# Block numbers earlier and in small portions, result stores from ScalarE's queue

## The reference

```python
shared = gelu(x2 @ Ws1 + bs1) @ Ws2 + bs2
y = shared
y = y + _bank_residual(x2, Wr_sp, br_sp, W1_sp, b1_sp, W2_sp, b2_sp)
y = y + _bank_residual(x2, Wr_fq, br_fq, W1_fq, b1_fq, W2_fq, b2_fq)
# _bank_residual, 8 experts, each 512 -> 128 -> 512, no row is over capacity here:
expert = argmax(softmax(x2 @ Wr + br)); gate = its probability
h = gelu(buf[expert] @ W1[expert] + b1[expert])
y = (h @ W2[expert] + b2[expert]) * gate
```

## Time and profile before

| | |
|---|---|
| median of 3 runs | 516.19 us |
| profiled execution | 513.78 us, span 512.0 us |
| TensorE busy | 458.2 us (89%), 2602 matmuls |
| VectorE, ScalarE, GpSimd busy | 212.8, 167.4, 176.0 us |
| DMA | 121.37 MB, mean 237 GB/s |
| y_dram<-ybuf | 18 stores of 256 KB, median 7.9 us to landing |
| x_raw<-x_dram | 12 loads of 256 KB |
| got<-y_dram | 10 gathers, GpSimd idle 43.0 us before them, 40.3 of it for a store of ybuf |

### The profile page before, as it was taken

One profiled execution on the slowest core, in us unless ns is written; L12 is line 12 of the kernel. 1 busy time (PEld: TensorE's weight loads), 2 busy tenths in 40 slices (PEclk: granted clock), 3 DMA queues, 4 the chain that ended last, 5 costly groups with the idle time before them and its releaser, 6 DMA issues.

```text
span 512.0 us, 7417 instructions
## 1 busy us (share of the span) xinstructions
PE 458.2 (89%) x2602; PEld 321.3 (63%) x2602; DVE 212.8 (42%) x518; ACT 167.4 (33%) x365; POOL 176.0 (34%) x198
## 2 busy tenths in 40 slices
PE   2799799989999998889999999999999996998980
PEld 2354447767665654666577877777777784864660
DVE  4779971212451728452221012420025595422226
ACT  2699673313210112720231032340064502243300
POOL 3102000083500802495325825206036339500081
PEclk9999999999999999999999999999999999999986
DMA  5999999969999879777504460210011016999965
GB/s 122 397 424 419 426 424 357 324 236 321 408 396 426 303 239 424 298 260 244 196 1 123 164 246 1 38 69 5 1 58 45 0 31 200 321 390 405 402 172 162
DMA packets 40164, 121.37 MB, mean 237 GB/s; under 512 B 7402, under 2 KB 7463, under 8 KB 31678
## 3 DMA queue, kind: packets, MB, share of 16 engines
q1 hardware_dynamic: 36766, 117.01, 61.0%
q0 software_dynamic: 3360, 3.86, 2.9%
HBM read 106.02 MB, written 14.82 MB: 236 GB/s over the span
## 4 chain that ended last, share of the span: by engine, by line
PE 70%; issue 9%; DVE 5%; POOL 5%; DMA 4%; ACT 3%; DVEq 1%; SPq 1%; POOLq 0%
PE ps L1601 13%; PE ps L1603 11%; PE ps L1602 11%; PE ps L1625 10%; PE ps L1960 9%; PE ps L1686 5%; PE ps L1805 2%; DMA y_dram<-ybuf 2%; ACT h_tmp L1347 1%; POOL sort L817 1%; DMA x_raw<-x_dram 1%; PE ps L2075 1%; POOL x_dram L846 1%; PE ps L1609 1%; DMA got<-y_dram,slot_u 1%
## 5 line engine op out<-in xcount | busy, mean ns | idle before, releaser
L1625 PE MATMUL ps<-ring,sel_att 128*32 128x512 f32 x512 | 66.0, 602 | 6.0 <-DMA ring<-in_L_gnn_basis_dram 2.4
L1601 PE MATMUL ps<-piece_hi,ht_hi 128*125 128x512 f32 x140 | 56.1, 401 | 0.8 <-PE ps L1603 0.6
L1602 PE MATMUL ps<-piece_lo,ht_hi 128*125 128x512 f32 x140 | 55.1, 394 | 0.0
L1603 PE MATMUL ps<-piece_hi,ht_lo 128*125 128x512 f32 x140 | 55.1, 394 | 0.0
L1084 DVE SCALAR_TENSOR_TENSOR u_lo<-ps,gates,u_hi 125x512 fp32r<-125x512 f32 x20 | 15.0, 751 | 94.1 <-ACT u_hi L1493 94.1
L751 POOL CAST piece_hi<-piece_raw 128x512 fp32r<-128x512 f32 x28 | 19.8, 707 | 92.3 <-issue 53.7
L752 POOL TENSOR_TENSOR piece_lo<-piece_raw,piece_hi 128x512 fp32r<-128x512 f32 x28 | 37.8, 1349 | 13.3 <-issue 11.1
L934 DVE TENSOR_SCALAR oh_n<-iota_n,keys 125x626 f16<-125x626 f16 x100 | 38.7, 387 | 7.9 <-PE ps L1686 5.7
L1960 PE MATMUL ps<-u_hi,cf 125*125 125x512 f32 x100 | 39.9, 399 | 1.3 <-PE ps L1603 1.3
L1960 PE MATMUL ps<-u_lo,cf 125*125 125x512 f32 x100 | 39.4, 394 | 0.0
L1686 PE MATMUL ps<-oh_n,oh_m 125*128 125x313 f16 x200 | 31.3, 314 | 4.3 <-DVE oh_m L935 4.3
(11 more groups left out here) (332 smaller groups left out, 934.9 us busy)
## 6 DMA issues: line engine op xcount, KB each, us to landing
ring<-in_L_gnn_basis_dram SPq DMA_DIRECT2D x64, 1024.0 KB, 9.4
w_home<-in_L_ffn_W_sp_dram SPq DMA_DIRECT2D x27, 256.0 KB, 5.6
y_dram<-ybuf SPq DMA_DIRECT2D x18, 256.0 KB, 7.9
rel_dram<-stag SPq DMA_DIRECT2D x16, 256.0 KB, 8.3
w_raw<-rel_dram SPq DMA_DIRECT2D x8, 512.0 KB, 6.4
piece_raw<-in_L_mix_Wkqv_dram SPq DMA_DIRECT2D x3, 1024.0 KB, 10.6
x_dram<-stag SPq DMA_DIRECT2D x1, 3072.0 KB
w_home<-in_L_ffn_W_fq_dram SPq DMA_DIRECT2D x12, 256.0 KB, 5.9
```

Of the source, the lines that this page charges most:

```text
L1601: pe.matmul(target, a_hi, b_hi, start=first, stop=False, skip_group_check=skip)
L1602: pe.matmul(target, a_hi, b_lo, start=False, stop=False, skip_group_check=skip)
L1603: return pe.matmul(target, a_lo, b_hi, start=False, stop=last, skip_group_check=skip)
L1625: last = pe.matmul(ps[32 * c:32 * c + 32, rel_bank(ch), :], sel_att[:, ch // CHUNKS, g].rearrange("p r q -> p (r q)"), ring[slot][:, c * D ...
```

## The change

On VectorE the numbers of the blocks are made directly behind the slots; the three selections pick(0), pick(1) and pick(2), which stood between the steps of routing, come behind the transposed routes. ScalarE reads the first four numbers of bank 1 only after the Gelus of three tiles, and one number more in each loop turn. SyncE reads its numbers four at a time between weight loads, and three groups of weights come ahead of the row loads. The stores of bank 0's seven tiles and of bank 1's first seven blocks are issued by ScalarE in the loop; SyncE keeps the last five of bank 1. SyncE's `load_w2` comes one turn sooner.

```diff
--- before.py
+++ after.py
@@ -472,6 +472,11 @@
         def rel_bank(ch):
             return 3 + ch % 2 if ch < 2 * CHUNKS - 2 else 3
 
+        def store_block(queue, b, i):
+            queue.wait_ge(*y_done(b, i))
+            n = SB_FQ if b else y_rows(i)
+            queue.dma_start(y_dram[b][i * 128:i * 128 + n, :], ybuf[b][0:n, i, :]).then_inc(y_out[b], 16)
+
         block = ctx.enter_context(nc.Block())
 
 
@@ -585,10 +590,6 @@
             for n, a in enumerate((b2_sp, b2_fq)):
                 sp.dma_start(out_bias[n * E:(n + 1) * E, :], a).then_inc(smalls_in, 16)
             sp.dma_start(out_bias[2 * E:2 * E + 1, :], bs2.rearrange("(a n) -> a n", a=1)).then_inc(smalls_in, 16)
-            def store_block(b, i):
-                sp.wait_ge(*y_done(b, i))
-                n = SB_FQ if b else y_rows(i)
-                sp.dma_start(y_dram[b][i * 128:i * 128 + n, :], ybuf[b][0:n, i, :]).then_inc(y_out[b], 16)
             sp.wait_ge(zeroed, ZEROED)
             for n in range(RAWS, len(UNITS)):
                 load_unit(n)
@@ -638,37 +639,38 @@
                 sp.dma_start(x_raw[i % XRAWS][:], x_dram[i * SB_FQ:(i + 1) * SB_FQ, :]).then_inc(raw_in[i % XRAWS], 16)
             expert_of = {0: load_numbers(0, 4)}
             load_w2(0)
-            fq_of = load_numbers(NB, 4) + load_numbers(NB + 4, 4) + load_numbers(NB + 8, 4)
-            for i in range(3):
+            fq_of = load_numbers(NB, 4)
+            for i in range(4):
                 load_w1_fq(i)
+            expert_of[1] = load_numbers(4, 4)
+            load_w2(1)
             for i in range(XRAWS):
                 load_rows(i)
-            for i in range(3, W1S):
+            fq_of += load_numbers(NB + 4, 4)
+            for i in range(4, W1S):
                 load_w1_fq(i)
             for i in range(4, W2S):
                 load_w2_fq(i)
-            for j in range(1, NY):
-                expert_of[j] = load_numbers(4 * j, y_rows(j) // SB)
-            load_w2(1)
-            load_w2(2)
+            fq_of += load_numbers(NB + 8, 4)
+            for j in range(2, 4):
+                expert_of[j] = load_numbers(4 * j, 4)
+                load_w2(j)
             for i in range(4):
                 load_w2_fq(i)
+            for j in range(4, NY):
+                expert_of[j] = load_numbers(4 * j, y_rows(j) // SB)
             for i in range(XRAWS, NB_FQ):
                 load_rows(i)
                 if i - XRAWS + W1S < NB_FQ:
                     load_w1_fq(i - XRAWS + W1S)
-                if i - 2 < NY:
-                    load_w2(i - 2)
+                if i - 1 < NY:
+                    load_w2(i - 1)
                 if i >= XRAWS + 3:
                     load_w2_fq(i - XRAWS - 3 + W2S)
-                    store_block(0, i - XRAWS - 3)
-                    store_block(1, i - XRAWS - 3)
-            for i in range(NB_FQ - XRAWS - 3, NB_FQ):
-                if i + W2S < NB_FQ:
-                    load_w2_fq(i + W2S)
-                if i < NY:
-                    store_block(0, i)
-                store_block(1, i)
+            for i in range(NB_FQ - XRAWS - 3, NB_FQ - W2S):
+                load_w2_fq(i + W2S)
+            for i in range(NY, NB_FQ):
+                store_block(sp, 1, i)
             for t in range(NT):
                 sp.wait_ge(final_ready, t + 1)
                 for a, b in ROWS:
@@ -1177,8 +1179,6 @@
             own_step(dve.tensor_reduce(denom[:].rearrange("p t b -> p (t b)"), flat(expo), AX.X, ALU.add))
             own_step(dve.reciprocal(gate_p[:], denom[:]))
             dve.tensor_tensor(flat(route), hot_flat, over(gate_p[:]), ALU.mult).then_inc(route_ready, 1)
-            pick(0)
-
             dve.wait_ge(route_mm, 1)
             count_all = scratch(TP, NT * 2 * E, 2 * E)
             above, need = scratch(TP, 96, 2 * E, STEPS), scratch(TP, 416, 2 * E)
@@ -1195,7 +1195,6 @@
             own_step(dve.tensor_tensor(by_bank(ahead), need.rearrange("p (b e) -> p b e", b=2).unsqueeze(2).to_broadcast([TP, 2, E, E]),
                                        lower_e[:], ALU.mult))
             own_step(dve.tensor_reduce(first_block[:], ahead, AX.X, ALU.add))
-            pick(1)
             for b, size in enumerate((SB, SB_FQ)):
                 dve.scalar_tensor_tensor(out=past_block[:, b * E:(b + 1) * E], in0=need[0:1, b * E:(b + 1) * E], scalar=float(size),
                                          in1=first_block[0:1, b * E:(b + 1) * E], op0=ALU.mult, op1=ALU.add).then_inc(dve_own, 1)
@@ -1207,18 +1206,19 @@
             dve.tensor_scalar(slot_u[:].rearrange("p t b -> p (t b)"), slot_f, -1.0, None, ALU.add).then_inc(slots_ready, 1)
             n[0] += 1
             dve.wait_ge(dve_own, n[0])
-            dve.wait_ge(route_tr, 1)
-            own_step(dve.tensor_copy(route_t[0:2 * E, 0:4 * TP], ps[0:2 * E, 0, 0:4 * TP]))
-            own_step(dve.tensor_copy(route_t[0:2 * E, 4 * TP:NODES], ps[0:2 * E, 1, 0:TP]))
-            own_step(dve.tensor_scalar(hot_t[:, 0:4 * TP], ps[0:2 * E, 0, 0:4 * TP], 0.0, None, ALU.is_gt))
-            dve.tensor_scalar(hot_t[:, 4 * TP:NODES], ps[0:2 * E, 1, 0:TP], 0.0, None, ALU.is_gt).then_inc(route_t_ready, 1)
-            pick(2)
             for b, at, count in ((0, 0, NB), (1, NB, NB_FQ)):
                 step = dve.tensor_tensor(passed[:, at:at + count, :], past_block[:, b * E:(b + 1) * E].unsqueeze(1).to_broadcast([1, count, E]),
                                          block_id[:, at:at + count].unsqueeze(2).to_broadcast([1, count, E]), ALU.is_le)
             own_step(step)
             own_step(dve.tensor_reduce(block_e, passed, AX.X, ALU.add))
             dve.tensor_scalar(block_ei[:], block_e, E - 1.0, None, ALU.min).then_inc(slots_ready, 1)
+            dve.wait_ge(route_tr, 1)
+            own_step(dve.tensor_copy(route_t[0:2 * E, 0:4 * TP], ps[0:2 * E, 0, 0:4 * TP]))
+            own_step(dve.tensor_copy(route_t[0:2 * E, 4 * TP:NODES], ps[0:2 * E, 1, 0:TP]))
+            own_step(dve.tensor_scalar(hot_t[:, 0:4 * TP], ps[0:2 * E, 0, 0:4 * TP], 0.0, None, ALU.is_gt))
+            dve.tensor_scalar(hot_t[:, 4 * TP:NODES], ps[0:2 * E, 1, 0:TP], 0.0, None, ALU.is_gt).then_inc(route_t_ready, 1)
+            for m in range(3):
+                pick(m)
 
             def rest_of_rows(t):
 
@@ -1568,10 +1568,11 @@
                     skip_runtime_bounds_check_because="VectorE limits each number to 0 .. E - 1 where it makes it")
                 return list(experts)
             unit_round(E, len(UNITS))
+            for t in range(NT - 2):
+                gated_rows(t)
             act.wait_ge(slots_ready, 2)
-            fq_of = load_numbers(NB, 4) + load_numbers(NB + 4, 4) + load_numbers(NB + 8, 4)
-            for t in range(NT - 1):
-                gated_rows(t)
+            fq_of = load_numbers(NB, 4)
+            gated_rows(NT - 2)
             take_turned(0)
             gated_rows(NT - 1)
             block_hidden(0)
@@ -1587,6 +1588,11 @@
                 if i - 2 < NY:
                     take_block(0, i - 2)
                 take_block(1, i - 2)
+                if 0 <= i - 3 < NY:
+                    store_block(act, 0, i - 3)
+                    store_block(act, 1, i - 3)
+                if i + 2 < NB_FQ:
+                    fq_of += load_numbers(NB + i + 2, 1)
             take_block(1, NB_FQ - 2)
             take_block(1, NB_FQ - 1)
             for h in range(2):
```

## The result

| | median, us | runs | ratio to before, 95% interval |
|---|---|---|---|
| before | 515.67 | 20 | |
| after | 512.38 | 20 | 0.9953 [0.9931, 0.9975] |
| after, second set | 514.17 | 12 | 0.9977 [0.9949, 1.0005] |
| after, third set | 514.14 | 12 | 0.9970 [0.9944, 0.9995] |

The change makes the kernel faster by 0.2 to 0.5%: the 44 runs of after lie on average 2.0 us under the runs of before timed beside them, where 4.9 were forecast. One run of E3 (519.60) is over 1.5% above that kernel's fastest and is left out of its ratio, not of its median.

A forecast was written before the change was run, and what follows sets the result against it. Bounds: waits around TensorE before the loop, and DMA at 404 GB/s within it. First gather at 480.8 instead of 485.67 saves 4.9 us: 508.9 from the profile, 511.3 from the median; forecast 510.3 between, 80% range 504.5 to 515.5.

The forecast's parts named there:

- Gap at TensorE, 5.9 us: Before the first sort matmul: the idle gap closes, 4.6 us, and the half-clock matmuls behind it go, 1.3 us.
- Block numbers near 416: On VectorE, with the picks moved away: block numbers ready near 416.0 us instead of 420.6.
- ScalarE's loads of 0.3 us: In the loop, each single-number load on ScalarE costs 0.3 us; bounds 0.29 and 4.86.
- rival D: Slower: ScalarE's number loads cost 4.5 us each in the loop, 532 us in all; decides from 1.2 us; chance 0.08.
- 4.4 us earlier all through: SyncE's load stream starts 0.8 us later with eight transfers less, so loop runs 4.4 us earlier; bounds 2.2 and 5.9.
- The sum: Last bank 0 store issued 474.8, landing 5.7, then 0.3: first gather at 480.8 instead of 485.67, gain 4.9 us.
- a wait moves, and I add nothing: x_raw 7 and 8 queue behind four second weights each on SyncE: charged nothing, 1 us as the other end.
- The last store, 5.7 us to landing: Bank 0's last store, on ScalarE's queue, lands 5.7 us after issue, the middle between 2.5 and 8.9.
- my good end of 2.5: Best case for the landing of bank 0's last store: 2.5 us, as on an idle queue.
- Bank 1's stores "in time": SyncE's last bank 1 store lands by 484.2 us, before the sixth gather at about 487.
- Rival B: SyncE's loads and issues all at their slowest: x_raw at 438.3, gathers at 486.0, 514.1 us; chance 0.13.
- Rival A: Stores on ScalarE's queue land no sooner, 8.5 us: gain 2.1, 511.7 by the profile, 514.1 by the median; chance 0.15.

The follow-up runs named there:

- E3: After, with bank 1's second weights ahead of bank 0's groups 2 and 3, and bank 0's last group three x_raw loads later: median 514.65 us, ratio 0.9982.
- P1: Before, with only ScalarE's first three Gelus put ahead of its block number loads: medians 517.34 and 517.57 us, ratios 1.0045 and 1.0054.
- E5: After, with SyncE's old load order restored behind the first twelve weights: medians 512.35 and 512.52 us, ratios to before 0.9946 and 0.9963.
- S1: After, with all result stores back on SyncE's queue: median 516.27 us, ratio to before 1.0012.
- P4: Before, with only the stores of bank 0 and of seven blocks of bank 1 moved to ScalarE's queue: median 516.15 us, ratio 1.0018.
- E7: E5, with SyncE reading its first twelve block numbers ahead of all twelve weight transfers: median 512.68 us, ratio to before 0.9960.

## Why the prediction was wrong

- **Gap at TensorE, 5.9 us.** Right: closed, full clock behind it, first transpose of x_raw 6.1 us ahead. P1 shows what it is worth alone: nothing.
- **Block numbers near 416 (4.3 us after the count).** Right: 4.2. x_raw was issued 21.4 us after the count, forecast 433.0 - 411.69 = 21.3.
- **ScalarE's loads of 0.3 us.** Right enough: 0.28 to 0.72 in the loop, 1.1 for the first. In the loop rival D's 1.2 us a load was not reached.
- **"4.4 us earlier all through" for the DMA stream, and with it the loop.** This is the step that failed. The sum is: issue of bank 0's last store, its landing, 0.3 us to the first gather. From the count on that was forecast as 63.1 (474.8 - 411.69) + 5.7 + 0.3 = 69.1 and measured as 69.6 + 2.2 + 0.3 = 72.1. The loop, forecast 4.4 us earlier at its end, was 2.0 later, by the means of all profiles 1.2. All profiles, in us after the count:

| | before (4) | after (3) | E5 (2) | S1 | P4 |
|---|---|---|---|---|---|
| last x_raw transpose starts | 67.4, 68.2, 68.2, 67.5 | 69.4, 69.8, 67.8 | 66.9, 65.9 | 67.8 | 70.3 |
| bank 0's last store issued | 64.8, 68.4, 67.4, 65.5 | 69.6, 70.0, 68.0 | 67.1, 66.1 | 67.9 | 70.5 |
| it takes to land | 8.9, 6.1, 7.0, 8.3 | 2.2, 2.2, 2.7 | 2.9, 3.5 | 6.2 | 2.9 |
| first gather starts | 74.0, 74.8, 74.8, 74.1 | 72.1, 72.5, 71.0 | 70.3, 69.9 | 74.3 | 73.7 |

  The lead in bytes was there at 28 us, 4.7 us of stream. Two things took it. First the order: I had seen that x_raw 7 and 8 stand behind four second weights each and wrote "a wait moves, and I add nothing", and did not see group 3 come in front of bank 1's first second weights. Between after and E5 this is 2.6 us at the last transpose and 2.3 of the stage. Second the stores: the forecast let them share the engines only for their own landing and charged the loads nothing. These are the queues over the first 61 us after the count, with packets, MB and share (q1 is SyncE's, q10 ScalarE's); before, after, E5, P4:

```profile
q1 hardware_dynamic: 8512, 15.52, 70.1%
```

```profile
q1 hardware_dynamic: 7881, 14.37, 67.5%
q10 hardware_dynamic: 1055, 1.93, 8.7%
```

```profile
q1 hardware_dynamic: 8118, 14.80, 67.5%
q10 hardware_dynamic: 1152, 2.10, 8.9%
```

```profile
q1 hardware_dynamic: 7557, 13.78, 61.4%
q10 hardware_dynamic: 1049, 1.92, 8.2%
```

  By then SyncE's queue is 1.15 MB behind before's in after and 0.7 MB in E5 (before's has stores in it, of which one of 0.26 MB had landed). What leads is stores: 1.93 MB, 4.8 us of a stream of 405 GB/s, which before stood for the most part behind the loads. P4, with nothing but the stores moved, shows the price: its last transpose is 2.1 to 2.9 us later than before's. After against S1 it is 1.2, less than after's own spread. The two prices together come near the 5.6 us that are missing (4.4 earlier forecast, 1.2 later measured); that they add is not shown, since the old order with the stores on SyncE was not run.

  E5's stage gain of 3.9 to 4.5 us lies near the sum's 4.9, but by other terms: its loop ends 1.4 us earlier and not 4.4, and the store lands in 2.9 and 3.5 us instead of 5.7. That is luck.
- **The last store, 5.7 us to landing.** It took 2.16, better than my middle and even than my good end of 2.5, since SyncE's queue had little left by then: from 482 to 486 us it moved 0.22 MB, ScalarE's 0.79. All that the stage gained came from here, since the loop ended no earlier: without the stores on ScalarE (S1) nothing is gained at all.
- **Bank 1's stores "in time".** No. The last one went at 489.94 and landed 6.3 us later amid the gathers; the sixth gather waited 2.57 us for it. The tail as a whole stayed at 26.3 us.
- **Rival B (SyncE is late).** SyncE was slow: one number load of 5.34 us and 4.47 us for four issues. x_raw still went on time, because it waited for GpSimd's weight split, as before.
- **Rival A (stores share the engines and land no sooner).** Its numbers, a gain of 2.1 us and 514.1 by the median, came nearer than mine, by luck: its landing of 8.5 us is refuted by 2.2. Its mechanism is half right. In after, the queues of SyncE (q1) and ScalarE (q10) from 462 to 464 us, with packets, MB and share:

```profile
DMA packets 442, 0.81 MB, mean 404 GB/s; under 512 B 48, under 2 KB 48, under 8 KB 442
...
q1 hardware_dynamic: 233, 0.41, 53.6%
q10 hardware_dynamic: 209, 0.40, 51.1%
```

Both queues together move the 404 GB/s that one moved before, half each: a store that lands sooner makes a load land later, which P4 shows as time. By the Trainium skill, page "DMA: Bandwidth & Descriptors", section "Issuing engines are not separate DMA queues", all issuers share the same 16 DMA engines; this window agrees. By the same page, "Queues, rings and completion order", a DMA engine takes turns between the queue rows that it has work for; the 233 and 209 packets agree. It did not begin at once: two stores were issued at 458.40, and from 456 to 460 only q1 moved, 892 packets, and up to 462 still q1 alone.

The forecast of a gain held, the size did not: 510.3 us was forecast, medians of 512.4 to 514.2 came.

## What to carry to other kernels

Bytes moved early count only as far as the order behind them stays right, and as far as they are the bytes that the bounding engine waits for: count them queue by queue. For each load that is moved ahead in a queue, write down what it is now in front of, when that is needed, and whether the moved load can stand in a wait of its own, since all loads behind it stand with it. A store that gets a queue of its own lands sooner at the price of the loads that stood ahead of it; set both in the sum. Closing a gap on the busiest engine (P1) or speeding the last store (P4) alone gave nothing while the DMA stream set the loop; the parts paid only together. And take the time of a changed stage from a mark inside the trace, over several profiles.

## What the hardware showed unexpectedly

In untouched code at 111 us TensorE waits 2 to 3.3 us for GpSimd. Then it either goes on at 2.4 GHz or runs slower for some microseconds, and all that follows is later. The wait's length does not decide it. Before (the second profile), timeline and window from 112 to 115:

```profile
111.67 0.41 PE L1601 MATMUL ps<-ht_hi,piece_hi 128*128 128x314 f32 x1 [2.01 <-POOL piece_lo L752]
...
112.00:115.00 3.00, 3.00 (x23) 3.00 (x22) 0.00 (x0) 0.00 (x0) 2.77 (x4) 1.00 0.76 184
```

E7:

```profile
111.64 0.41 PE L1606 MATMUL ps<-ht_hi,piece_hi 128*128 128x314 f32 x1 [2.01 <-POOL piece_lo L753]
...
112.00:115.00 3.00, 3.00 (x14) 3.00 (x13) 0.00 (x0) 0.00 (x0) 2.78 (x4) 0.50 0.64 213
```

The same wait of 2.01 us, then a clock of 1.00 and 23 matmuls, or 0.50 and 14. One and the same VectorE instruction behind it starts at 117.61 us and at 119.11. Three of four profiles of before kept the full clock, one of the fourteen of all other kernels (E3's). Whether that is chance or hangs on something in the program is open. A second place adds to it, whose cause I did not find: between the same two VectorE instructions, near 202 and 253 us, ten profiles take 51.1 to 51.2 us and eight 52.3 to 52.5. The first place bears on the result: in the profiled executions of before and after the instruction above starts at 117.42 and 119.71 us, the whole 2.3 us by which the count of after is later. It may also be why E5's timed runs show less than its stage.
